# A fused attention and routed-FFN block on one core: three VectorE operations and one GpSimd split change their pairs

## The reference

```python
h = layernorm(x) * (1 + ca) + sa
q, k, v = ((h @ W + bias).reshape(b, 16, 32, t) for W, bias in ...)
attn = softmax(einsum('bhdt,bhds->bhts', k, v) * temperature)   # over s
x = x + ga * einsum('bhdt,bhts->bhds', q, attn).reshape(b, t, d)
h = layernorm(x) * (1 + cb) + sb
scores = h @ w_router
top, idx = top_k(scores, 512)          # half of the tokens of each batch
f = gelu(h[idx] @ W1 + b1) @ W2 + b2
x = x + gb * (h with sigmoid(top) * f added at idx)
```

## Time and profile before

| | |
|---|---|
| median of three runs | 2418.35 us (2418.11 to 2418.71) |
| profiled execution | 2416.8 us |
| its span, first to last instruction | 2415.1 us |
| mean granted clock of TensorE | 0.984 |
| PE busy | 2273.9 us, 94% |
| DVE busy | 1911.6 us, 79% |
| ACT busy | 1478.1 us, 61% |
| POOL busy | 1371.5 us, 57% |
| row maxima (L981), 1024 | 1212.6 us, 1215 ns each |
| exponentials (L810), 1024 | 1136.7 us, 1114 ns each |
| router products (L1010), 66 | 89.4 us, 1355 ns each |
| qn (L1042), 257 | 96.9 us, 377 ns each |

### The profile page before, as it was taken

One profiled execution on the slowest core, in us unless ns is written; L12 is line 12 of the kernel. 1 busy time (PEld: TensorE's weight loads), 2 busy tenths in 40 slices (PEclk: granted clock), 3 DMA queues, 4 the chain that ended last, 5 costly groups with the idle time before them and its releaser, 6 DMA issues.

```text
span 2415.1 us, 41301 instructions
## 1 busy us (share of the span) xinstructions
PE 2273.9 (94%) x12772; PEld 887.0 (37%) x12772; DVE 1911.6 (79%) x2806; ACT 1478.1 (61%) x2616; POOL 1371.5 (57%) x1205
## 2 busy tenths in 40 slices
PE   6999999999999999999999999897989999999996
PEld 2333333333333333333333333231334444444442
DVE  5899899999999999999999999998744543554432
ACT  1788888888888888888888887777311111111110
POOL 4566676666756667666666666554344452543531
PEclk9999999999999999999999999999999999999998
DMA  6233333233333333323233333223612021111100
GB/s 214 68 92 77 79 82 88 72 91 72 76 87 77 84 73 90 82 70 96 67 80 97 72 79 75 67 61 97 157 44 66 22 59 52 32 57 44 57 23 18
DMA packets 123771, 180.83 MB, mean 75 GB/s; under 512 B 44112, under 2 KB 44112, under 8 KB 123480
## 3 DMA queue, kind: packets, MB, share of 16 engines
q1 hardware_dynamic: 113760, 152.30, 25.8%
q0 software_dynamic: 9728, 25.23, 3.4%
HBM read 67.17 MB, written 43.16 MB: 46 GB/s over the span
## 4 chain that ended last, share of the span: by engine, by line
PE 64%; DVE 17%; issue 8%; POOL 5%; ACT 3%; DMA 2%; SPq 1%; DVEq 0%; POOLq 0%; ACTq 0%
PE sc L558 13%; PE acc L605 13%; PE sc L747 12%; PE sc L734 12%; DVE nmax L981 10%; PE pj L568 7%; PE pj L580 5%; POOL x L1320 3%; DVE qn L1042 2%; ACT probs L810 2%; DVE stats L1024 1%; DMA room<-in_L_ffn_W 1%; PE sc L591 1%; POOL sel_rows L120 1%; DVE rinv L1037 1%
## 5 line engine op out<-in xcount | busy, mean ns | idle before, releaser
L810 ACT ACTIVATE probs<-sc,nmax 128x1024 f32<-128x1024 f32 x1024 | 1136.7, 1114 | 276.2 <-DVE nmax L981 254.8
L981 DVE TENSOR_REDUCE nmax<-sc 128x1 f32<-128x1024 f32 x1024 | 1212.6, 1215 | 61.1 <-PE sc L558 55.1
L605 PE MATMUL acc<-probs,qn 128*32 128x512 f32 x4136 | 556.7, 611 | 9.8 <-DVE x L1019 7.3
L883 ACT ACTIVATE probs<-sc,b_col 128x512 f32<-128x512 f32 x128 | 87.9, 687 | 561.6 <-PE sc L734 498.7
L568 PE MATMUL pj<-room 128*128 128x512 f16 x1536 | 395.6, 381 | 0.4 <-ACT qT L800 0.4
L747 PE MATMUL sc<-room,probs 128*128 128x512 f16 x1536 | 353.9, 380 | 8.0 <-DVE probs L1171 8.0
L558 PE MATMUL sc<-room 128*128 128x512 f16 x1024 | 310.3, 385 | 38.3 <-ACT probs L810 27.9
L558 PE MATMUL sc<-stacks 128*128 128x512 f16 x1024 | 309.5, 384 | 31.4 <-ACT probs L810 30.8
L1169 DVE CAST probs<-probs 128x512 f16<-128x512 f32 x128 | 64.6, 505 | 332.6 <-ACT probs L883 315.9
L747 PEld LDWEIGHTS sc<-room,probs 128*128 128x128 f16 x1536 | 150.0, 98 | 190.5 <-issue 7.4
L568 PEld LDWEIGHTS pj<-room 128*128 128x128 f16 x1536 | 150.2, 98 | 188.2 <-issue 9.1
(11 more groups left out here) (147 smaller groups left out, 2369.2 us busy)
## 6 DMA issues: line engine op xcount, KB each, us to landing
room<-room SPq DMA_DIRECT2D x512, 64.0 KB, 2.0
stacks<-room SPq DMA_DIRECT2D x512, 64.0 KB
h_rows<-hbuf SPq DMA_DIRECT2D x132, 128.0 KB, 2.3
out<-base SPq DMA_DIRECT2D x132, 128.0 KB, 2.5
room<-in_L_attn_x SPq DMA_DIRECT2D x96, 128.0 KB, 2.7
rows<-mod_rows SPq DMA_DIRECT2D x32, 256.0 KB, 4.1
room<-in_L_ffn_W SPq DMA_DIRECT2D x8, 1024.0 KB, 5.2
probs<-in_L_wmod SPq DMA_DIRECT2D x4, 1024.0 KB, 7.9
```

The source lines that it names most:

```text
L605: mm = nc.tensor.matmul(acc[at:at + DH, :], qn[:, (p // 2) % 2, p % 2, h2, :], probs[:, (2 * p + h2) % PROBS, half * D:(half + 1) * D], st ...
L810: nc.scalar.activation(probs[:, u % PROBS, :], slot(g, ring_at(p, h2)), ACT.Exp, bias=nmax[:, u % PROBS:u % PROBS + 1], accum_out=rsum[:, ...
L883: nc.scalar.activation(g32[:, f % 2, :], ff[f % 2], ACT.Gelu_apprx_tanh, bias=b1_col[:, f:f + 1], scale=1.0 / WS).then_inc(gelu_done, 1)
L981: nc.vector.tensor_reduce(nmax[:, u % PROBS:u % PROBS + 1], slot(g, ring_at(p, h2)), AX.X, ALU.max, negate=True).then_inc(max_done, 1)
```

## The change

DVE's extra operations of a group move: the second `stats_of_x2` and `aggregate2` from pair 6 to 7; the second `stats_of_x` from 11 to 13 and `aggregate` from 11 to 14; `dot_router(0)` from pair 13 to 15; `dot_router(1)` from pair 15 to pair 1 of the next group, and one more call after the last group. For the product that now runs in the next group (and once before there is anything to multiply) the table of scores begins with four spare columns in place of two (`AHEAD`), and those that read it or wait for its semaphore follow. POOL's second K split goes from behind the residual (portion of pair 4) to the portion of pair 6, ahead of `normed_before`. In the last batch four steps of the ranking and of the weights move by one to four pairs.

```diff
+AHEAD = 2 * SUBS
...
-        self.scores = sb("scores", [P, 2 * NG + 2])
+        self.scores = sb("scores", [P, AHEAD + 2 * NG])
...
-            sp.wait_ge(s_dot, 2 * NG + 2)
+            sp.wait_ge(s_dot, 2 * NG + 3)
...
-                        if last and g == 1 and p == 0:
-                            act.wait_ge(s_dot, 2 * (NG - 3))
+                        if last and g == 1 and p == 2:
+                            act.wait_ge(s_dot, 2 * (NG - 3) + 1)
...
-                                               accum_out=scores[:, bass.ds(b * (2 * GB) + 2 * g + s, 1)]).then_inc(s_dot, 1)
+                                               accum_out=scores[:, bass.ds(b * (2 * GB) + 2 * g + s + SUBS, 1)]).then_inc(s_dot, 1)
...
-                if g == 0 and p == 7:
+                if g == 0 and p == 6:
...
-                if g == 1 and p in (2, 7, 10, 14):
+                if g == 1 and p in (2, 6, 10, 14):
                     count_above(nc, dve, r, 3 + p // 4, only)
-                if g == 1 and p == 1:
+                if g == 1 and p == 5:
                     weights(slice(0, LAST * TB), 1)
...
-                        if p == 5 or p == 6:
-                            stats_of_x2(b, g, p - 5)
-                        if p == 6:
+                        if p == 1:
+                            dot_router(1, b, g - 1)
+                        if p == 5 or p == 7:
+                            stats_of_x2(b, g, (p - 5) // 2)
+                        if p == 7:
                             aggregate2(b, g)
-                        if (p == 9 or p == 11) and load:
+                        if (p == 9 or p == 13) and load:
                             if p == 9:
                                 dve.wait_ge(s_xhat, b * GB + g + 3)
-                            stats_of_x((g + 3) % 4, (p - 9) // 2, b * 64 + 64 * ((g + 3) // 4 + 1))
-                        if p == 11 and load:
+                            stats_of_x((g + 3) % 4, (p - 9) // 4, b * 64 + 64 * ((g + 3) // 4 + 1))
+                        if p == 14 and load:
                             aggregate(b * GB + g + 4)
-                        if p == 13 or p == 15:
+                        if p == 15:
                             dve.wait_ge(s_hm, b * (3 * GB) + 3 * g + 2)
-                            dot_router((p - 13) // 2, b, g)
+                            dot_router(0, b, g)
...
             gated(B, -1, 1)
+            dot_router(1, B, -1)
...
                     residual(b, g)
+                    behind_qn(b, g, 3)
                     if not end:
                         split_kv(nxt, 1, n4 + 2)
-                    behind_qn(b, g, 3)
                     normed_before(b, g)
```

More of the change, by code:

```diff
@@ L457, in store_scores @@
                 with nc.allow_non_contiguous_dma(reason="4 byte scores, a few thousand in all"):
-                    sp.dma_start(score_rows[k].rearrange("(t p) -> p t", p=P), scores[:, bass.ds(k * TB + 2, TB)]).then_inc(s_sc, 16)
+                    sp.dma_start(score_rows[k].rearrange("(t p) -> p t", p=P), scores[:, bass.ds(k * TB + AHEAD, TB)]).then_inc(s_sc, 16)
             def load_scores(bat):
@@ L848, in body @@
                             evac_q((g + 1) % 2, (p - 13) // 2, n2 + (p - 13) // 2 + 1)
-                        if last and g == 1 and p == 0:
-                            act.wait_ge(s_dot, 2 * (NG - 3))
-                            nc.scalar.activation(r.e_neg[:, 0:LAST * TB], scores[:, 2:2 + LAST * TB], ACT.Exp, scale=-1.0).then_inc(s_exps, 1)
+                        if last and g == 1 and p == 2:
+                            act.wait_ge(s_dot, 2 * (NG - 3) + 1)
+                            nc.scalar.activation(r.e_neg[:, 0:LAST * TB], scores[:, AHEAD:AHEAD + LAST * TB], ACT.Exp, scale=-1.0).then_inc(s_exps, 1)
                         if end and p == 3:
@@ L891, in ffn @@
                     if first and f == 6:
-                        act.wait_ge(s_dot, 2 * NG + 2)
-                        nc.scalar.activation(r.e_neg[:, LAST * TB:], scores[:, 2 + LAST * TB:], ACT.Exp, scale=-1.0).then_inc(s_exps, 1)
+                        act.wait_ge(s_dot, 2 * NG + 3)
+                        nc.scalar.activation(r.e_neg[:, LAST * TB:], scores[:, AHEAD + LAST * TB:], ACT.Exp, scale=-1.0).then_inc(s_exps, 1)
                     if first and f == 7:
@@ L1080, in rank_first @@
             def rank_first(g, p):
-                if g == 0 and p == 7:
-                    nc.vector.tensor_copy(r.s8[:], scores[:, 2:2 + TB]).then_inc(s_s8, 1)
+                if g == 0 and p == 6:
+                    nc.vector.tensor_copy(r.s8[:], scores[:, AHEAD:AHEAD + TB]).then_inc(s_s8, 1)
                     dve.wait_ge(s_s8, 1)
@@ L1157, in count_tile @@
                     if t == 0:
-                        nc.vector.tensor_copy(r.s8[:], scores[:, bass.ds(nb * (2 * TB) + npar * TB + 2, TB)]).then_inc(s_s8, 1)
+                        nc.vector.tensor_copy(r.s8[:], scores[:, bass.ds(nb * (2 * TB) + npar * TB + AHEAD, TB)]).then_inc(s_s8, 1)
                         dve.wait_ge(s_s8, count(1, 1))
```

## The result

The kernel with the change takes 2391.95 us (median of 4 runs, 2388.49 to 2394.73), beside 2418.23 for the kernel before on the same chip (4 runs, 2417.39 to 2418.71): a ratio of 0.9897, 95% interval 0.9882 to 0.9913. The profiled execution of after took 2388.49 us, the shortest of its four, so that differences between the two traces come out some 2 us larger than those of the medians.

A forecast was written before the change was run, and what follows sets the result against it. PE was taken to bound the attention loop, with a 0.97 us stall per group. 28 x (0.44 - 0.07) = 10.4, less 1.8, plus 1.5, gave 10.1 us: 2408 from the median, stated as 2407, range 2394 to 2418.

The forecast's parts named there:

- Part 1: x2 statistics and aggregate to pair 7: the stall before pair 8 moves to pairs 9 to 11, gaining nothing alone.
- Part 2: Second K split behind pair 6's qn: that qn loses 0.60 of waiting; pair 11 starts 0.44 us earlier per group.
- The wait of pair 8's qn: Pair 8's qn may wait for POOL's normalization step L1281: 0.15 us taken, bounds 0 and 0.63.
- Part 3, second product: Router product at the next group's pair 1: waits about 0.17 for POOL, delays pair 4's qn, costs 0.07 us per group.
- The 1.8 us forecast behind the jumps: First group after each of six jumps: pair 1's product meets L1281's full first step, costing 6 x 0.3 us.
- Part 3, first product: Router product from pair 13 to 15: saves 1.3 us on DVE, worth nothing in PE's time.
- Part 4: Second x statistics from pair 11 to 13, aggregate to 14: no PE stall near either place, worth 0.
- The last batch: Batch after the loop: shorter qn waits against later ranking work, a gain of 1.5 us, bounds -2 and +4.
- A: Rival: all of pair 8's stall goes because DVE catches up, 28 x 0.97 = 27 us, 2391; chance 0.12.
- B: Rival: waits swap places, pair 1's product and pair 8's qn each meeting L1281, 2414 to 2418; chance 0.16.
- C: Rival, slower: pair 1's router product takes 1.99 instead of 0.68 us behind POOL, 2438; chance 0.12.

The follow-up runs named there:

- e2_stats2_alone: Kernel before with only the second statistics and the aggregate of x2 moved to pair 7: 2419.46 us, ratio 1.0015.
- e9_split_and_dots: Kernel before with only the second K split behind pair 6's qn and the router products at pair 15 and the next group's pair 1: 2391.23 us, ratio 0.9912.
- e1_split_alone: Kernel before with only the second K split moved behind pair 6's qn: 2402.14 us, ratio 0.9949.
- e7_first_stats_at_6: Kernel after with the first statistics of x2 between the two maxima of pair 6: 2383.74 us, ratio 0.9873.
- e5_two_at_13: Kernel after with 1.26 us of useless DVE work at pair 13 in the last group of each loop batch: 2401.55 us, ratio 0.9945.

## Why the prediction was right inside the group and wrong at the jump

**Part 1**, "gains nothing", is what e2_stats2_alone and e9_split_and_dots measured: groups of 48.98 and 48.56 against 48.99 and 48.55. The stall moved to the pairs named.

**Part 2**, 0.44 per group: 0.55 by e1_split_alone. The wait of pair 8's qn, taken at 0.15 between the bounds 0 and 0.63, was 0.34 - 0.29 = 0.05, which is 0.10 of the 0.11 between forecast and result. The replications on SP stayed covered.

**Part 3, second product**, 0.07 per group: 0.10 to 0.12 (48.55 against 48.44, and 49.11 against 48.99). The product took 0.85 against 0.68 beside a lone one, the 0.17 that was worked out. The 1.8 us forecast behind the jumps didn't come: there the product takes 0.68 at all six places, meeting no step of POOL, and the first group behind a jump lasts 48.45, the shortest of all. The sum of parts 2 and 3 inside the groups is 28 x 0.45 = 12.6 by the plain group's gain, 13.3 by the table; forecast were 10.4 less 1.8.

**Part 3, first product: this step failed.** I wrote that PE's pairs there show no stall, "so the 1.3 us saved on DVE is worth nothing in PE's time", and of the jump that it is one "which the change does not touch". Both rest on the same reading: PE's stall at the jump, read with "issue" as its releaser, was taken for a constant. The saved 1.3 us of DVE shorten six jumps by 1.2 on average, 7.1 us, and the clock that stays up behind them is worth 6.5. Together 13.6 us, which the sum put at nothing. The profiled executions differ by 28.3, 18.2 more than the 10.1 of the sum; the rest of these 18.2 is 4.7 in the groups (13.3 where 10.4 less 1.8 was forecast) and the 1.3 at the loop's start, less the 1.5 forecast for the last batch, whose 0.7 was lost again behind it. The trace of before held two hints. Of its six jumps only three have "issue" as the releaser; the other three name ACT's exponential (one is the 267.13 row above), though all six are alike. And DVE's 1.99 product, with an exponential that ends only 0.18 ahead of PE's last score product, stands in front of each.

**Part 4** is worth nothing in time, as said, but it has a side effect that the prediction didn't see: pair 12's qn now meets the last step of a V split and takes 1.12 instead of 0.29 (the 839.31 row; 0.29 in e9_split_and_dots, where no statistics move). There DVE has the room; in the stretch from pair 6 to 9 the same meeting cost 0.60 per group. **The last batch** gave 0.7 for the forecast 1.5, inside its bounds.

**The rivals.** A gave 2391, the number that came, but by luck, since its mechanism didn't: its stall at pair 11 is still 0.60, groups last 48.55 and not 48.03, and the statistics alone gain nothing. B's meetings took place but cost 0.05 and 0.17. C's product of pair 1 takes 0.68 to 0.86 throughout the loop, never near 1.99.

## What to carry to other kernels

In this kernel the loop's jump costs PE an instruction fetch, which begins only once the last wait in the body is over. So the work of the other engines that this wait hangs on has an earlier deadline than in any other place, although no product of the body is late: keep it light in the last pairs, and put what is left behind it (1.26 us of DVE work cost 11.6 us ahead of it and 1.7 behind). Inside a stretch where an engine works without a break, moving its work gains nothing; taking away what blocks it (the split beside qn) or starting the stretch earlier (e7_first_stats_at_6) does.

## What the runs showed of the hardware

- From the start of the 16 KB instruction packet to PE's first product behind the jump it is 2.7 to 3.5 us, of which 0.93 to 1.70 is the packet itself and 1.65 to 1.87 follows (66 jumps). Where DVE is late at all jumps alike (before), the packet's length makes most of the differences between them. Where nothing is late the packet starts 0.12 to 0.23 after pair 15's second product at 32 of 42 jumps, and 0.3 to 1.0 after it at the other ten; why, and what the 1.7 consists of, no run shows.
- The granted clock fell to half behind 18 of the 26 jumps whose stall was 2.02 to 2.96 us and behind none of the 40 whose stall was 1.06 to 1.98, each drop costing 1.3 to 1.8 us. The stall alone doesn't settle it (in e5_two_at_13 it fell behind one of 2.12 and not behind those of 2.37 and 2.80), so the runs of one kernel spread by about such drops.
- DVE's qn of pair 6 takes 0.29 with POOL idle and 0.89 beside its last split step. The Trainium skill ("SBUF — State Buffer", section "SBUF: two separate sides") has a DVE instruction with two SBUF inputs and a GpSimd one that reads SBUF exclude each other for the whole instruction; the rows of after agree, since the 0.60 went with the meeting.
